# State-space layer, routed experts and gated feed-forward on one core: epsilon added on GpSimd, the count of blocks by two additions, new task orders

## What is computed

```python
delta = softplus(x @ Wd + bd);  B = x @ WB + bB;  C = x @ WC + bC;  A = -exp(A_log)
h = clip(exp(min(delta*A, 2)) * h + clip(delta*B, -2, 2) * x, -100, 100)   # scan over tokens, 16 states
y = sum(h * C) + x * D_param
routing = softmax(y @ Wr + br);  e = argmax(routing)                       # 4 experts, top 1
moe = (silu(y @ up_w[e] + up_b[e]) @ down_w[e] + down_b[e]) * max(routing)
a = layernorm(y + moe) * ln_w + ln_b                                       # first norm
x1 = layernorm(x + a)                                                      # second norm
out = layernorm(x1 + (silu(x1 @ wg) * (x1 @ wu)) @ wdn)                    # third norm, wg, wu, wdn = int / 127
```

## Time and profile before

| | |
|---|---|
| median of 3 runs | 1034.03 us (1033.85 to 1037.81) |
| the profiled execution, its own time | 1039.55 us |
| its span, first to last instruction | 1037.4 us |
| PE / DVE / ACT / POOL busy, share of the span | 68% / 71% / 56% / 57% |
| mean granted TensorE clock | 0.793 of full speed |
| chain that ended last, by engine | PE 33%, DVE 18%, issue 14%, ACT 12%, POOL 12%, DMA 9% |

### The profile page before, as it was taken

How to read it: one execution, slowest core, us unless ns; L and a number is a source line. 1 busy time by engine, 2 the same in 40 slices (tenths; PEclk the granted TensorE clock), 3 DMA queues, 4 the chain that set the end, 5 groups by cost and what they waited for, 6 DMA issues and landing times.

```text
span 1037.4 us, 14202 instructions
## 1 busy us (share of the span) xinstructions
PE 704.3 (68%) x4320; PEld 547.1 (53%) x4320; DVE 732.9 (71%) x1334; ACT 576.2 (56%) x1060; POOL 593.9 (57%) x468
## 2 busy tenths in 40 slices
PE   2445748864997388937995699649974896278144
PEld 1233527642875267726773487427762675167133
DVE  2799886589878987899788987898789853211031
ACT  6560637493767476656768476937562663235122
POOL 1365475268836794578637873679367835430440
PEclk8665858885999589966997599859985898579666
DMA  3433456734574447543674456445734482126100
GB/s 90 141 125 103 125 183 207 217 112 150 181 245 138 163 137 229 196 151 107 226 217 150 129 178 221 139 150 171 254 116 163 140 250 92 56 82 189 38 1 20
DMA packets 82061, 155.06 MB, mean 149 GB/s; under 512 B 9392, under 2 KB 51120, under 8 KB 81968
## 3 DMA queue, kind: packets, MB, share of 16 engines
q1 hardware_dynamic: 69168, 140.89, 42.3%
q0 software_dynamic: 4096, 8.40, 2.7%
q10 hardware_dynamic: 8704, 4.72, 1.7%
HBM read 138.56 MB, written 15.40 MB: 148 GB/s over the span
## 4 chain that ended last, share of the span: by engine, by line
PE 33%; DVE 18%; issue 14%; ACT 12%; POOL 12%; DMA 9%; SPq 1%; DVEq 0%; ACTq 0%; POOLq 0%
DVE state L1064 7%; PE psT L609 7%; PE psU L596 5%; PE psD L650 5%; DMA weights<-in_w_pack 4%; PE psY L490 3%; POOL prod L1091 3%; ACT decay L720 3%; DVE bst L1020 3%; PE psT L606 2%; DMA y_sorted<-rows_in 2%; PE psU L634 2%; POOL rows_in L1112 2%; PE psB L484 2%; POOL chosen_out L1120 2%
## 5 line engine op out<-in xcount | busy, mean ns | idle before, releaser
L1091 POOL TENSOR_TENSOR prod<-state,c_wide 128x1024 f32<-128x1024 f32 x128 | 301.2, 2358 | 229.8 <-DVE state L1064 218.0
L484 PE MATMUL psB<-parts,sel 128*128 128x512 bf16 x256 | 113.5, 462 | 170.1 <-DVE state L1064 168.6
L1055 DVE TENSOR_TENSOR psB<-dx,psB 128x512 f32<-128x512 f32 x256 | 168.1, 688 | 54.9 <-PE psB L484 48.3
L1064 DVE TENSOR_TENSOR_SCAN state<-decay,state,psB 128x512 f32<-128x512 f32 x128 | 163.8, 1280 | 14.0
L490 PE MATMUL psY<-ident,prod 128*128 128x128 f32 x1024 | 162.4, 315 | 8.1 <-POOL prod L1091 8.1
L490 PEld LDWEIGHTS psY<-ident,prod 128*128 128x128 f32 x1024 | 145.5, 166 | 21.4 <-POOL prod L1091 11.1
L1064 DVE TENSOR_TENSOR_SCAN state<-decay,psB 128x512 f32<-128x512 f32 x128 | 155.2, 1213 | 1.9 <-ACT decay L720 1.9
L720 ACT ACTIVATE decay<-delta,a_sb 128x1024 f32<-128x1024 f32 x128 | 139.7, 1140 | 28.0 <-DVE state L1064 25.8
L484 PEld LDWEIGHTS psB<-parts,sel 128*128 128x128 bf16 x256 | 26.6, 104 | 217.8 <-DVE state L1064 215.9
L759 ACT ACTIVATE hid<-psU,weights 128x128 f32<-128x128 f32 x352 | 100.4, 369 | 69.0 <-PE psU L596 67.0
L596 PE MATMUL psU<-yT_sorted,weights 128*128 128x128 f32 x704 | 98.9, 287 | 9.4 <-DMA weights<-in_w_pack 5.9
(11 more groups left out here) (138 smaller groups left out, 1181.8 us busy)
## 6 DMA issues: line engine op xcount, KB each, us to landing
c_wide<-c_rows SPq DMA_DIRECT2D x128, 512.0 KB, 4.6
weights<-in_w_pack SPq DMA_DIRECT2D x88, 578.0 KB, 4.5
xT_sb<-in_xT SPq DMA_DIRECT2D x8, 512.0 KB, 3.9
y_sorted<-rows_in SPq DMA_DIRECT2D x16, 256.0 KB, 5.1
...
```

What stands on the lines that cost most here:

```text
L484: pe.matmul(tokens(psB, c, h), sel[:, s, :], parts[:, c.n % 2, h * HALF:h * HALF + c.hw], start=True, stop=True).then_inc(b_ready, 1)
L1055: v.tensor_tensor(tokens(psB, c, h), dx[:, n % 2, h * HALF:h * HALF + c.hw], tokens(psB, c, h), ALU.mult).then_inc(inp_ready, 1)
L1064: v.tensor_tensor_scan(state[:, g % NSTATE, t0:t0 + c.hw], decay[:, g % NDECAY, t0:t0 + c.hw], tokens(psB, c, h), before, ALU.mult, ALU.ad ...
L1091: g_.tensor_tensor(prod[:, g % NPROD, w], state[:, g % NSTATE, w], c_wide[:, g % NC, w], ALU.mult).then_inc(prod_ready, 1)
```

## The change

Three things are changed.

1. The epsilon is added by POOL, at the head of `rstd`, from a constant tile `eps` that is set once. DVE's `tensor_scalar` L1028 is gone. POOL's power now waits for the sum and for minus the mean.
2. The running count is made by two `tensor_tensor` additions: `pairs` = each number plus its left neighbour, then `first_block` = each pair plus the one two places to the left. Both tiles have zeros ahead. `ones_e` is gone; four small memsets are new in the set-up.
3. All five tables are written anew.

```diff
-SETUP = 17
+SETUP = 21
...
 PE_ORDER = [
-    (0, "spread", 1, 0), (0, "spread", 1, 1), (-1, "yT_turn"), (1, "z"), (-1, "logits"), (0, "skip"),
+    (0, "spread", 2, 0), (-1, "yT_turn"), (0, "spread", 2, 1), (0, "skip"), (-1, "logits"), (0, "spread", 3, 0),
...
+            setup(v.memset(eps[:, 0, :], EPS))
+            setup(v.memset(eps[:, 1, :], EPS * 127.0 * 127.0))
+            setup(v.memset(pairs[:, :], 0.0))
+            setup(v.memset(n_blocks[:, :], 0.0))
...
-                    v.tensor_reduce(n_blocks[:, :], over_size[:, :, :], X, ALU.add).then_inc(slot_steps, 1)
-                    dve.wait_ge(slot_steps, 5 * n + 2)
-                    v.tensor_tensor_scan(first_block[:, 1:1 + E], ones_e[:, :], n_blocks[:, :], 0.0, ALU.mult, ALU.add
-                                         ).then_inc(slot_steps, 1)
+                    v.tensor_reduce(n_blocks[:, 1:1 + E], over_size[:, :, :], X, ALU.add).then_inc(slot_steps, 1)
+                    dve.wait_ge(slot_steps, 6 * n + 2)
+                    v.tensor_tensor(pairs[:, 2:2 + E], n_blocks[:, 1:1 + E], n_blocks[:, 0:E], ALU.add
+                                    ).then_inc(slot_steps, 1)
+                    dve.wait_ge(slot_steps, 6 * n + 3)
+                    v.tensor_tensor(first_block[:, 1:1 + E], pairs[:, 2:2 + E], pairs[:, 0:E], ALU.add
+                                    ).then_inc(slot_steps, 1)
...
-                    dve.wait_ge(stats_steps[h], 6 * turn + 2 * k + 1)
-                    v.tensor_scalar(ve[:, h, 0:c.hj], mv[:, h, 0:c.hj, 1], EPS if k < 2 else EPS * 127.0 * 127.0, None,
-                                    ALU.add).then_inc(stats_steps[h], 1)
...
-                    pool.wait_ge(stats_steps[h], 6 * turn + 2 * k + 2)
+                    pool.wait_ge(stats_steps[h], 3 * turn + k + 1)
                     wait(pool, normed[h], 3 * turn + k)
+                    g_.tensor_tensor(ve[:, h, hj], mv[:, h, hj, 1], eps[:, int(k == 2), hj], ALU.add
+                                     ).then_inc(rstd_steps, 1)
                     g_.tensor_tensor(minus_mean[:, h, hj], mv[:, h, hj, 0], minus_one[:, hj], ALU.mult
                                      ).then_inc(rstd_steps, 1)
+                    pool.wait_ge(rstd_steps, 2)
                     g_.tensor_tensor(rstd[:, h, hj], ve[:, h, hj], minus_half[:, hj], ALU.pow).then_inc(rstd_steps, 1)
-                    pool.wait_ge(rstd_steps, 2)
+                    pool.wait_ge(rstd_steps, 3)
```

More of the change, by code:

```diff
@@ new lines @@
+    (0, "spread", 5, 0), (0, "spread", 5, 1), (-1, "rank"), (0, "add", 2), (0, "add", 3), (0, "spread", 6, 0),
+    (0, "spread", 6, 1), (0, "spread", 7, 0), (0, "add", 4), (0, "spread", 7, 1), (-2, "x_turn", 0),
+    (-2, "x_rest", 0), (0, "add", 5), (-2, "ff_up", 0, 0), (-2, "ff_up", 0, 1), (0, "spread", 8, 0),
+    (0, "spread", 8, 1), (1, "b_turn"), (-2, "ff_up", 0, 2), (-2, "ff_up", 0, 3), (-2, "ff_up", 0, 4),
+    (0, "spread", 9, 0), (0, "spread", 9, 1), (-2, "ff_up", 0, 5), (0, "add", 6), (0, "add", 7), (-1, "sort_turn", 0),
@@ L87 @@
+    (1, "spread", 1, 1), (2, "z"),
 ]
 ACT_ORDER = [
[L89 to L93 removed]
@@ L105 @@
-    (-2, "ff_mul", 1, 2), (0, "scan", 14), (-1, "router_pick"), (-2, "stats", 1, 2), (1, "flag"), (0, "scan", 15),
-    (1, "scan", 0), (1, "scan", 1), (0, "router_shift"), (1, "scan", 2), (1, "scan", 3), (1, "scan", 4), (0, "slots"),
-    (-1, "combine", 0), (-1, "stats", 0, 0), (1, "scan", 5), (1, "scan", 6), (-1, "stats", 0, 1), (1, "scan", 7),
-    (2, "delta"), (1, "scan", 8), (-1, "combine", 1), (-1, "stats", 1, 0),
+    (0, "scan", 8), (-2, "ff_mul", 0, 0), (-2, "ff_mul", 0, 1), (0, "scan", 9), (-2, "ff_mul", 0, 2), (1, "b_max"),
@@ new lines @@
+    (0, "scan", 10), (-2, "stats", 1, 1), (1, "bc_low"), (0, "scan", 11), (-2, "stats", 0, 2), (1, "bound", 0),
+    (0, "scan", 12), (0, "scan", 13), (1, "bound", 1), (1, "over"), (0, "scan", 14), (1, "dx"), (-2, "ff_mul", 1, 0),
+    (-2, "ff_mul", 1, 1), (-2, "ff_mul", 1, 2), (-2, "stats", 1, 2), (-1, "router_pick"), (1, "flag"),
+    (0, "scan", 15), (1, "scan", 0), (1, "scan", 1), (1, "scan", 2), (0, "router_shift"), (1, "scan", 3),
+    (1, "scan", 4), (-1, "combine", 0), (-1, "stats", 0, 0), (1, "scan", 5), (0, "slots"), (1, "scan", 6),
@@ L109 @@
+    (-1, "stats", 0, 1), (-1, "combine", 1), (1, "scan", 7), (-1, "stats", 1, 0), (2, "delta"),
 ]
 POOL_ORDER = [
-    (0, "bound_input"), (-1, "prod", 10), (-3, "rstd", 0, 2), (-1, "prod", 11), (-1, "prod", 12), (-1, "prod", 13),
-    (-1, "prod", 14), (-3, "rstd", 1, 2), (-1, "prod", 15), (0, "prod", 0), (0, "prod", 1), (-2, "gather", 0),
-    (-2, "gather", 1), (-2, "gather", 2), (-2, "gather", 3), (-2, "gather", 4), (-2, "gather", 5), (0, "prod", 2),
-    (-2, "gather", 6), (-2, "gather", 7), (0, "prod", 3), (-2, "rstd", 0, 0), (0, "prod", 4), (-2, "affine", 0),
@@ L115 @@
-    (-1, "scatter", 0), (0, "prod", 5), (-2, "rstd", 0, 1), (-1, "scatter", 1), (-1, "scatter", 2),
+    (0, "bound_input"), (-1, "prod", 10), (-1, "prod", 11), (-3, "rstd", 0, 2), (-1, "prod", 12), (-1, "prod", 13),
+    (-3, "rstd", 1, 2), (-1, "prod", 14), (-1, "prod", 15), (0, "prod", 0), (-2, "gather", 0), (0, "prod", 1),
+    (-2, "gather", 1), (-2, "gather", 2), (-2, "gather", 3), (-2, "gather", 4), (-2, "gather", 5), (-2, "gather", 6),
+    (-2, "gather", 7), (0, "prod", 2), (0, "prod", 3), (0, "prod", 4), (-2, "rstd", 0, 0), (-2, "affine", 0),
@@ L116 @@
+    (0, "prod", 5), (-1, "scatter", 0), (-2, "rstd", 0, 1), (-1, "scatter", 1), (-1, "scatter", 2),
     (-1, "scatter", 3), (-1, "scatter", 4), (-1, "scatter", 5), (-1, "scatter", 6), (-1, "scatter", 7),
-    (0, "prod", 6), (0, "prod", 7), (-2, "rstd", 1, 0), (1, "bc_rest"), (-2, "affine", 1), (0, "prod", 8),
-    (0, "prod", 9), (-2, "rstd", 1, 1),
+    (-2, "rstd", 1, 0), (0, "prod", 6), (0, "prod", 7), (1, "bc_rest"), (0, "prod", 8), (0, "prod", 9),
+    (-2, "affine", 1), (-2, "rstd", 1, 1),
@@ L126 @@
-    (-1, "weights", 2),
[3 rows of a table added]
+    (-2, "weights", 8), (-2, "weights", 9), (-2, "weights", 10), (0, "c", 0), (0, "over"), (-2, "store", 1),
+    (1, "xT"), (0, "c", 1), (0, "c", 2), (-2, "store", 2), (0, "c", 3), (0, "c", 4), (0, "c", 5), (-1, "weights", 0),
+    (-1, "weights", 1),
 ]
```

72 lines of the change are left out of this document (29 added, 43 removed), and 3 rows, old and new, of the table SP_ORDER.

## The result

The changed kernel takes 1067.1 us (median of 4 runs, 1055.97 to 1068.67), the kernel before 1034.73 us beside it (4 runs, 1033.85 to 1037.81). The ratio of the means is **1.0284, 95% interval 1.0211 to 1.0357**: slower by some 3%, where the forecast was 997 us, 3.6% faster. The profiled execution took 1068.67 us, its span is 1066.9 us.

The account below looks back on a forecast made before the run. DVE was taken to bound 50 us of each iteration, PE 60. Terms -4.35 - 2.3 - 1.79 + 0 + 2.35 gave -6.1 us per iteration, -36.7 in all with the ends: 1002.9, or 997 us against the median; range 972 to 1030.

Parts of the forecast that it names:

- A microsecond taken from DVE in its own 50 us can shorten the iteration.: Two parts of each iteration, 50 us together, were held to be bound by DVE's scans, busy 44.76 us there.
- The step from the chain to the sum, -4.35 us per iteration: Waits of `ve` behind POOL's `prod`, shown as "issue" on the path, were to go: 4.35 us off each iteration.
- The 4.61 us wait, taken at 2.3: `ve` at 477.90, beside PE's `ff_up` chain: half of its 4.61 us wait was to come out, 2.3.
- The router, -1.79: DVE's wait for PE's `logits` was to be hidden, `router_shift` coming a scan later: 1.79 us off each iteration.
- The running count, 0: At `slots`, the two additions replacing the scan were to wait for `prod` just as the scan did: 0.
- `combine`, +2.35: `combine` 0, now straight behind scan 4, was to wait for one `prod`: 2.35 us more, bounds 0 and 4.68.
- The SP order moves two transfers by one place; the weights are fetched three blocks ahead: 0: SP's new table of transfers was to cost nothing: 0.
- nothing for `rstd` 1 0 on POOL: POOL's epsilon addition on the path through a `rstd` was put at 0, bound 0.9 us for six.
- slower: PE's line: PE's `x_turn` and `ff_up` ahead of `spread` 8 make scan 8 wait: about 1052 us, chance 0.08.
- The waits move to other instructions: Rival: `combine` 0 and `slots` both meet POOL's queue of products, handing back much gain: 1022 us, chance 0.22.
- what was to show it: Signs expected in the changed profile, among them DVE busy near 86 us and the iteration at about 104 us.

Follow-up runs that it names:

- e3_eps: The kernel before with only the epsilon added on POOL, all tables as before: 1031.83 us, ratio 0.9968.
- g3_combine_late: The changed kernel with `combine` 0 and `stats` 0 0 moved behind `slots` in DVE's table: ratio 1.0316.
- e5_pool_back: The changed kernel with POOL's order table of before: 1069.39 us, ratio 1.0373.
- h4_after_rows: The changed kernel with SP's table of before, and the `rows` transfer moved ahead of C row 9: 1038.09 us, ratio 1.0044.

## Why the prediction was wrong

It was wrong in sign, and two steps of it failed.

*"A microsecond taken from DVE in its own 50 us can shorten the iteration."* Here it shortened it by little. The busy times were right: e3_eps took the 8.7 us off DVE that the earlier trace rows gave. The step from the chain to the sum, -4.35 us per iteration, is what failed: e3_eps measured about -1.1. The chain of the earlier trace rows is one path among several that end close together, and its 2.05 us of "issue" at 464.68 was `prod` 5's time under another name. I had laid POOL's `prod` beside `ve`, but not asked what stands behind that `prod` on POOL: the very `rstd` that `ve` releases. And the 1.5 us by which `x_turn` 0 did come earlier end ahead of `up` 0, which ScalarE's copy held; the 1.1 us of the iteration are 1.7 gained behind `up` 0 less 0.6 lost ahead of it.

*The 4.61 us wait, taken at 2.3.* It gave nothing. In e3_eps it is 4.29 us for PE, and in the changed kernel DVE waits 2.6 to 3.2 us for `spread` 8, where it had not waited before.

*The router, -1.79.* The wait is gone at its place, and nothing in the time shows it. No run has it alone.

*The running count, 0.* Right in the time: `pairs` took 1.51 and 1.68 us on the old tables, and the runs gave 1.0019 and 1.0011. The Trainium skill's rule (GPSIMD Engine Reference, Specifications: two inputs from SBUF contend) had said so, and these traces agree. In the changed kernel 0.91 us at `pairs` and 0.64 more at `passed` add up to near the old wait, so the wait stays with `slots`, at another instruction.

*`combine`, +2.35.* The mechanism was right and its size small. One `combine` 0 of the kernel after, and the products beside it:

```profile
575.01 6.43 DVE L1010 SCALAR_TENSOR_TENSOR moe<-chosen_out,top_w,ytok 128x128 f32<-128x128 f32 x4 [0.44 <-DMA chosen_out<-rows_out,slot]
```
```profile
573.51 6.99 POOL L1095 TENSOR_TENSOR prod<-state,c_wide 128x1024 f32<-128x1024 f32 x3
```

It waited for three products at once, over 5 us, outside my bounds of 0 to 4.68; on the mean it is 3.8 us per chunk. But g3_combine_late and e5_pool_back show that this is not where the time went.

*"The SP order moves two transfers by one place; the weights are fetched three blocks ahead: 0", and nothing for `rstd` 1 0 on POOL.* This is the step that cost the sign. I had noted in the change that `rstd` 1 0 comes right after the scatters, and priced POOL's addition in it at 0. It puts `prod` 6 1.8 us later (489.40 to 491.20), `prod` 6 frees the buffer of C row 9, and SP has `rows` behind C row 9. The scatters end another 1.7 us later in the new tables. The old tables had `rows` behind `prod` 6 too, but there ScalarE's copy came last, 0.7 us behind what `rows` would have allowed in the kernel before and 1.3 us in e3_eps; the new ACT and POOL tables took that cover away. The ratio 1.0284 stands for 29 us (the medians are 32 apart), and about 20 of them go when `rows` alone is moved. That `rstd` 1 0 and the later scatters share them half and half is read from the rows; no run moves either alone. Of the rest, the other moves on SP may be 0.3 to 0.5% (1.0232 against 1.0284, 1.0044 against 1.0078, intervals that overlap); they are more than the prediction counted, with `weights` 3 now ahead of C rows 10 and 11 and `store` 0 ahead of C row 13. What remains from 1.0044 to the 1.0011 of the old tables is 3 us, again with intervals that overlap, and I have no run that names it.

Of the rivals, "slower: PE's line" had the sign and not the cause: it put the loss on `x_turn` ahead of `spread` 8, worth 1052 us. The wait at scan 8 is there, but h4_after_rows keeps that order and that wait (2.6 to 3.2 us) and is within 0.5% of before. "The waits move to other instructions" describes DVE well and the time not at all.

Of what was to show it: DVE busy near 86 us (88.14), the iteration at 104 (114 to 117.6), `pairs` near 1.8 or 0.17 (0.91), the first `combine` over 3 us (yes), the router's wait gone (yes), DVE idle under 3 us ahead of scan 8 (2.6 to 3.2).

Open remains what holds the 47 us between `up` 0 and scan 15 on the old tables: with the epsilon on POOL it is 1.7 us shorter (48.3 to 46.6), while `up` 0 comes 0.6 us later. In e3_eps the last scatter already ends 0.8 us later, with POOL's additions in the same queue, which may be that loss and is not tested.
